# Fused transformer stack on one core: the second cross-attention gets folded query square sums, an earlier begin and a new order of its groups, its first group and its tail

## The chip, the cores and the metric

One core of one Trainium2 chip runs the whole program in one launch. The metric is the device time in microseconds (us). Below, PE is TensorE, DVE is VectorE, ACT is ScalarE, POOL is GpSimd and SP the engine that issues the DMAs.

## The reference

Six sublayers work on x (16 batches of 64 tokens, 512 wide), each followed by a layer norm of x plus its result. The fifth, the one this change is about, is a cross-attention with normalised queries and keys (cut):

```python
q = (hidden_states @ q_proj_w.T).reshape(B, Q, NUM_HEADS, HEAD_DIM).transpose(0, 2, 1, 3)
k = (cross_attention_states @ k_proj_w.T).reshape(B, KV, NUM_KV_HEADS, HEAD_DIM).transpose(0, 2, 1, 3)
v = (cross_attention_states @ v_proj_w.T).reshape(B, KV, NUM_KV_HEADS, HEAD_DIM).transpose(0, 2, 1, 3)
q = rmsnorm(q, q_norm_w)        # w * x * rsqrt(mean(x*x) + 1e-5), over the 128 of a head
k = rmsnorm(k, k_norm_w)
...
attn = jax.nn.softmax(scores + attention_mask, axis=-1)
out = jnp.einsum('bhqk,bhkd->bhqd', attn, v)
return out.transpose(0, 2, 1, 3).reshape(B, Q, NUM_HEADS * HEAD_DIM) @ o_proj_w.T
```

There are 32 query heads, 8 key/value heads of 128, keys and values come from a context `ctx_4096` (16 x 64 tokens) that doesn't depend on x. The fourth sublayer is a self-attention of the same size, the sixth a small gated mixture of low-rank experts.

## The kernel before

Stages follow one another: `attn0`, `xattn0`, `ffn0`, `attn1`, `xattn1` (the second cross-attention), `ffn1`. All values are float32. Large products are made as three matmuls of high and low parts (`mm3`, lines 263 to 265); small ones (scores, square sums) as true fp32 matmuls, each of which shows as two instructions.

An attention stage has 8 groups, one per key/value head with its 4 query heads. A group has 12 projection units, `U_0` to `U_11`. In `xattn1` the first four are key/value units (24 matmuls, context as the stationary side, 256 columns), which read only the context, and the other eight are query units (12 matmuls, 512 columns). `KT` transposes the normalised keys, `SQ` makes the square sums of the queries, `SC` scores of one pair of batches blocks, `TR`/`PT` carry the probabilities out to DRAM and back in turned order (DVE transpose, four DMAs out, one in, then a high/low split on ACT and DVE into `pth`, `ptl`), `PV` multiplies them with v, `WS` splits the output weights, `WO` (12 matmuls) projects a tile of 128 tokens out and adds it to X. Four pairs per group, numbered 0 to 3; eight `WO` tiles.

What sets the order is a string in `schedule`: each engine walks the same list and does its own share of every event, so the list is at once the order of PE, ACT and DVE. A dash behind an event means that it belongs to the group before. POOL and SP have orders of their own in `step` of `pool_attention` and `sp_attention`. Engines are tied by counting semaphores; each engine works in its own order, and a wait holds whatever stands behind it.

Square sums of the queries before: ACT writes the squares of a query unit to `sq` (line 690), PE multiplies eight 128 x 128 blocks of squares, as stationary side, with one column of ones (`square_sums`, line 576), DVE scales the eight columns (line 801), POOL takes the power -1/2 (line 971), and the scores are multiplied with it on DVE (line 816).

```python
for m in range(8):
    last = nc.tensor.matmul(pb[3][:, m:m + 1], sq[:, m, :], onecol[:, 0:1], start=True, stop=True)
```

Between `attn1` and `xattn1`, SP and POOL wait for the last addition to X (`stage_end`) before they load and split the first weights, and PE waits until all eight x tiles are normalised, transposed and split (`xt_ready`), although the key/value units don't read x. In the tail after the last group the remaining `PV` and `WO` run, each finished tile is normalised and transposed for the next stage, and POOL splits the weights of `ffn1` (line 1689).

## Time and profile before

| | us |
|---|---|
| median of 3 runs (2396.45 to 2406.70) | 2397.24 |
| profiled execution, its own time | 2401.77 |
| its span in the profile | 2400.0 |
| PE busy in the span | 2289.1 (95%) |
| DVE busy | 1206.0 (50%) |
| ACT busy | 780.5 (33%) |
| POOL busy | 765.6 (32%) |

Busy time of PE counts a matmul from its start to its modelled end, so matmuls overlap; the pace is read from the starts. The granted clock of PE is given as a share of full speed: 1.00 is the upper of two levels (2.4 GHz), 0.50 the lower (1.2 GHz), and a value between is a mix over the stretch. `[2.66 <-DVE otl L874]` behind a row: the engine sat idle for 2.66 us just before, and what ended it.

### The profile page before, as it was taken

The page shows a single profiled execution, that of the slowest core. Times are in us where ns is not written, and L with a number is a line of the kernel's source. Part 1 is how long each engine was busy: PE and PEld are TensorE (multiplying, and loading weights), DVE is VectorE, ACT ScalarE, POOL GpSimd, SP SyncE. Part 2 cuts the span into 40 slices and gives each one's busy share as a digit, 9 for nine tenths or more (in the row PEclk, how much of TensorE's full clock was granted, in tenths as well). Part 3 has the DMA queues.
Part 4 walks back from the last instruction along what each step waited for, and adds up shares of the span by engine and source line. Part 5 has one row for each costly group of instructions (what it writes and reads, how often), then busy time and mean ns, then how long its engine had stood idle before and what let it go on. Part 6 is the DMA issues. An engine that isn't in the chain of part 4 may idle for free. (4 is left out here: it accounts for less than half of the span.)

```text
span 2400.0 us, 34599 instructions
## 1 busy us (share of the span) xinstructions
PE 2289.1 (95%) x12210; PEld 1833.6 (76%) x12210; DVE 1206.0 (50%) x2052; ACT 780.5 (33%) x1475; POOL 765.6 (32%) x709
## 2 busy tenths in 40 slices
PE   8999999997999989998999999998899999999989
PEld 6888888875555557886788888887788888888867
DVE  3445544447677633334444444556345454544456
ACT  2233223223677731222322223332232233323321
POOL 4122222203333335444222222211443433333233
PEclk9999999998999999999999999999889999999989
DMA  4222222211000113311221222121121212211120
GB/s 160 80 66 60 76 79 79 57 45 32 18 18 11 64 70 123 105 52 54 81 80 50 67 75 78 56 53 49 59 80 54 57 48 79 67 43 53 53 75 36
DMA packets 120546, 152.43 MB, mean 64 GB/s; under 512 B 16272, under 2 KB 67984, under 8 KB 119952
## 3 DMA queue, kind: packets, MB, share of 16 engines
q1 hardware_dynamic: 120464, 151.33, 21.5%
q8 instruction: 52, 0.85, 0.1%
q14 instruction: 30, 0.25, 0.0%
HBM read 124.02 MB, written 27.26 MB: 63 GB/s over the span
## 5 line engine op out<-in xcount | busy, mean ns | idle before, releaser
L263 PE MATMUL banks<-xTh,wh 128*128 128x512 f32 x1024 | 418.7, 409 | 8.8 <-DVE xTl L1887 7.4
L265 PE MATMUL banks<-xTh,wl 128*128 128x512 f32 x1024 | 404.7, 395 | 0.0
L264 PE MATMUL banks<-xTl,wh 128*128 128x512 f32 x1024 | 403.6, 394 | 0.0
L263 PE MATMUL banks<-woh,oth 128*128 128x512 f32 x768 | 315.6, 411 | 23.3 <-DVE otl L874 16.4
L264 PE MATMUL banks<-wol,oth 128*128 128x512 f32 x768 | 302.5, 394 | 0.0
L961 POOL TENSOR_TENSOR sc_sb<-sc_sb,rs 128x512 f32<-128x512 f32 x96 | 104.3, 1090 | 621.1 <-DVE rs L837 621.1
L265 PE MATMUL banks<-woh,otl 128*128 128x512 f32 x768 | 302.1, 393 | 0.0
L880 DVE TENSOR_TENSOR X<-banks,X 128x512 f32<-128x512 f32 x192 | 132.7, 691 | 324.3 <-PE banks L265 323.9
L693 ACT ACTIVATE q_sb<-banks 128x512 f32<-128x512 f32 x192 | 114.5, 597 | 400.6 <-PE banks L265 400.6
L263 PEld LDWEIGHTS banks<-xTh,wh 128*128 128x128 f32 x1024 | 195.6, 191 | 51.0 <-issue 9.2
L265 PEld LDWEIGHTS banks<-xTh,wl 128*128 128x128 f32 x1024 | 194.9, 190 | 44.0
L264 PEld LDWEIGHTS banks<-xTl,wh 128*128 128x128 f32 x1024 | 195.9, 191 | 37.3
L564 PEld LDWEIGHTS banks<-k_sb,q_sb 128*128 128x128 f32 x1536 | 191.0, 198 | 19.0 <-ACT q_sb L693 6.7
L874 DVE TENSOR_TENSOR otl<-banks,oth 128x512 fp32r<-128x512 f32 x192 | 123.6, 686 | 158.6 <-ACT oth L733 158.6
L564 PE MATMUL banks<-k_sb,q_sb 128*128 128x64 f32 x1536 | 191.4, 279 | 9.5 <-ACT q_sb L693 4.1
L263 PEld LDWEIGHTS banks<-woh,oth 128*128 128x128 f32 x768 | 146.2, 190 | 69.3 <-DVE otl L874 17.9
L947 POOL TENSOR_TENSOR wl<-raw,wh 128x512 fp32r<-128x512 f32 x144 | 193.4, 1343 | 12.0
L945 POOL TENSOR_SCALAR wh<-raw 128x512 fp32r<-128x512 f32 x144 | 91.0, 632 | 314.1 <-DMA raw<-in_a_in 163.7
L265 PEld LDWEIGHTS banks<-woh,otl 128*128 128x128 f32 x768 | 145.9, 190 | 32.4
L264 PEld LDWEIGHTS banks<-wol,oth 128*128 128x128 f32 x768 | 146.4, 191 | 26.3
L733 ACT ACTIVATE oth<-banks 128x512 fp32r<-128x512 f32 x192 | 104.3, 596 | 124.1 <-PE banks L608 124.1
L690 ACT ACTIVATE sq<-banks 128x512 f32<-128x512 f32 x64 | 38.3, 598 | 242.7 <-PE banks L265 242.7
(208 smaller groups left out, 4039.9 us busy)
## 6 DMA issues: line engine op xcount, KB each, us to landing
raw<-in_a_in SPq DMA_DIRECT2D x144, 256.0 KB, 2.9
raw<-in_a_out SPq DMA_DIRECT2D x96, 256.0 KB, 2.7
turned<-pq SPq DMA_DIRECT2D x384, 64.0 KB, 2.0
pt<-turned SPq DMA_DIRECT2D x96, 256.0 KB, 2.9
f_q<-in_f_q SPq DMA_DIRECT2D x21, 512.0 KB, 3.9
f_s<-in_f_s SPq DMA_DIRECT2D x21, 512.0 KB, 5.3
X<-in_x SPq DMA_DIRECT2D x1, 2048.0 KB, 10.5
x_craw<-in_ctx SPq DMA_DIRECT2D x8, 256.0 KB, 2.7
```

The costliest lines, as they stand in the source:

```text
L263: nc.tensor.matmul(out, w_hi, x_hi, start=start, stop=False)
L264: nc.tensor.matmul(out, w_hi, x_lo, start=False, stop=False)
L265: return nc.tensor.matmul(out, w_lo, x_hi, start=False, stop=stop)
L564: last = nc.tensor.matmul(pb[2][:, (4 * c + m) * S:(4 * c + m + 1) * S], q_sb[:, 4 * (pair % 2) + m, c * P:(c + 1) * P], k_sb[:, col:col + S],
L690: nc.scalar.activation(sq[:, :, g % 2 * S:(g % 2 + 1) * S], bank[:, :].rearrange("p (c s) -> p c s", c=8), ACT.Square).then_inc(A["q_sq"], 1)
L693: nc.scalar.activation(q_sb[:, :, g * S:(g + 1) * S], bank[:, :].rearrange("p (c s) -> p c s", c=8), ACT.Copy).then_inc(A["q_free" if st.r ...
L733: nc.scalar.activation(oth[:, n % 2, :, 64 * b:64 * b + 64], PVB[b][:, :].rearrange("p (c s) -> p c s", c=8), ACT.Copy).then_inc(A["o_hi"], 1)
L874: nc.vector.tensor_tensor(otl[:, n % 2, :, half], PVB[b][:, :].rearrange("p (c s) -> p c s", c=8), f32(oth[:, n % 2, :, half]), ALU.subtra ...
L880: nc.vector.tensor_tensor(xtile(n), bank[:, :], xtile(n), ALU.add).then_inc(A["x_added"], 1)
L945: nc.gpsimd.tensor_scalar(hi, src, 1.0, 0.0, ALU.mult, ALU.add).then_inc(A["w_hi"], 1)
L947: nc.gpsimd.tensor_tensor(lo, src, f32(hi), ALU.subtract).then_inc(A["w_ready"], 1)
L961: nc.gpsimd.tensor_tensor(rows, rows, spread_rows(rs[:, pair, :]), ALU.mult).then_inc(A["p_ready"], 1)
```

## The change

1. **Square sums.** DVE transposes the squares in 32 x 32 blocks (`sq_turned`, 1024 elements a partition), reduces over 32 (`sq_part`, 32 a partition), and PE makes one fp32 matmul of a constant 128 x 128 matrix `fold` with these 32 columns. DVE then picks the columns that are a partition's own (`sq_pick`) and reduces by four. The event `SQ` is now the DVE transpose and reduce, and `SS` the matmul and the picking. Three small DVE instructions at the stage's begin build `fold` and its helpers.
2. **Begin.** `attn1`'s tail now holds `U_0` and `U_1` of `xattn1`'s first group, behind x tile 5's transposes and ahead of those of tiles 6 and 7, which go to other banks. SP loads the first weights as soon as `attn1` has used its own, POOL splits two chunks between norm roots, and only `U_4` waits for all x tiles.
3. **Order of a group.** In `xattn1`, `SC2`, `SC3` and `SS3` of a group run inside the next group, ahead of its `WO0`; the parts of the score work have events of their own (`SC` PE, `SD` DVE, `EX` ACT, `SU` DVE). The first group has one list for PE and another for ACT and DVE. POOL's and SP's orders follow, and in the tail the last scores move likewise; loads for `ffn1` are issued ahead of the last two turned pairs, and POOL's splits for it are put between the norm roots.
4. Two counters of the layer norm become one, and the counter of the outgoing transfers likewise, in all stages.

```diff
@@ schedule
     if rms:
-        ev = events("U_0 PT0- TR2- U_1 WS0- WS1- U_2 PV0- PT1- TR3- WS2- WS3- U_3 WO0- PV1- U_4 KT0 PT2- WO1- U_5 KT1 PV2- WO2- SQ0 "
-                    "U_6 PT3- U_7 WO3- SQ1 PV3- SC0 WO4- SC1 U_8 U_9 WO5- SQ2 TR0 U_10 U_11 TR1 WO6- SQ3 SC2 WO7- SC3")
+        ev = events("WS0- WS1- PT0- U_0 SS3- WS2- WS3- U_1 PV0- PT1- U_2 SC2- SD2- EX2- U_3 SU2- WO0- TR2- PV1- SC3- SD3- EX3- "
+                    "U_4 KT0 SU3- WO1- U_5 KT1 TR3- PT2- SQ0 U_6 PV2- SS0 U_7 WO2- PT3- SQ1 WO3- SS1 PV3- WO4- SC0 SD0 EX0 "
+                    "WO5- SU0 SC1 SD1 EX1 U_8 TR0 SU1 U_9 TR1 SQ2 WO6- U_10 SS2 U_11 SQ3 WO7-")
...
     if not project:
-        return events("PT0- TR2- PV0- WO6-- " + ("" if rms else "VT1- ") + "PT1- TR3- WO7-- WS0- WS1- PV1- WS2- WS3- WO0- PT2- WO1- "
+        if rms:
+            return events("PT0- PV0- WO6-- SS3- PT1- WO7-- WS0- WS1- SC2- SD2- WS2- WS3- EX2- SU2- PV1- SC3- TR2- WO0- SD3- EX3- "
+                          "SU3- WO1- TR3- WO2- PT2- WO3- PV2- WO4- PT3- WO5- PV3- WO6- WO7-")
...
+def first_group(rms, tensor):
+    if not rms:
+        return schedule(False, True, False)
+    if tensor:
+        return events("U_0 U_1 U_2 U_3 U_4 KT0 U_5 KT1 U_6 SS0 U_7 U_8 SC0 SS1 U_9 SC1 U_10 U_11 SS2")
+    return events("U_0 U_1 U_2 U_3 U_4 KT0 U_5 KT1 SQ0 U_6 SS0 U_7 SQ1 SS1 SD0 EX0 SU0 SD1 TR0 U_8 U_9 SQ2 EX1 SU1 TR1 "
+                  "U_10 U_11 SS2 SQ3")
@@ sp_attention
-            if st.before:
+            if st.name == "xattn1":
+                for name in ("w_ready", "wo_ready", "s_out"):
+                    sp.wait_ge(*st.at(name, 0))
+            elif st.before:
                 sp.wait_ge(*stage_end(st.before))
...
-                    if before and c in (1, 3):
+                    if before and c in (1, 3) and not st.rms:
                         move_out(i - 1, 2 + c // 2)
-                    if before and c in (2, 4):
+                    if before and c in (2, 4) and not st.rms:
                         move_in(i - 1, 1 + c // 2)
+                if before and st.rms:
+                    for pair in (2, 3):
+                        move_out(i - 1, pair)
+                        move_in(i - 1, pair)
@@ square_sums, PE
-                for m in range(8):
-                    last = nc.tensor.matmul(pb[3][:, m:m + 1], sq[:, m, :], onecol[:, 0:1], start=True, stop=True)
-                last.then_inc(A["ss_done"], 1)
+                nc.tensor.matmul(pb[3][:, 0:32], fold[:, 0:P], sq_part[:, j % 2, :], start=True,
+                                 stop=True).then_inc(A["ss_done"], 1)
@@ pe_attention, tail
+            if st.name == "attn1":
+                pe.wait_ge(const_set, 2)
+                pe.wait_ge(fs["c"], 4)
+                for u in range(2):
+                    pe.wait_ge(xt_ready, 8 * XT_NORMS["attn1"] + NT - 3 + u)
+                    pe_unit(pe, stages[2], 0, u)
@@ act_attention, query unit
+                    if isinstance(i, int) and (i, u) == (0, 8):
+                        st.need(act, "sc_done", 2)
-                    st.need(act, "ss_done", 4 * i + 2 * n + g // 2)
+                    st.need(act, "sq_turn", 4 * i + 2 * n + g // 2)
@@ dve_attention
+            def q_square_sums(i, j):
+                st.need(dve, "sq_sum", 4 * i + j)
+                st.need(dve, "q_sq", 8 * i + 2 * j + 2)
+                nc.vector.transpose(sq_turned[:, :, :].rearrange("p n d -> p (n d)"),
+                                    sq[:, :, :].rearrange("p m s -> p (m s)")).then_inc(A["sq_turn"], 1)
+                st.need(dve, "ss_done", 4 * i + j - 1)
+                st.need(dve, "sq_turn", 4 * i + j + 1)
+                nc.vector.tensor_reduce(sq_part[:, j % 2, :], sq_turned[:, :, :], AX_X, ALU.add).then_inc(A["sq_sum"], 1)
...
+                nc.vector.scalar_tensor_tensor(sq_pick[:, :, :], pb[3][:, 0:32].rearrange("p (m b) -> p m b", m=8), EPS,
+                                               own, ALU.add, ALU.mult).then_inc(A["sq_own"], 1)
@@ pool_attention, step of a stage with norms
                     if before:
+                        q_root(i - 1, 3)
+                    for n in range(3):
+                        k_root(i, n)
+                    if before:
                         normalise(i - 1, 2)
-                    k_root(i, 0)
-                    k_root(i, 1)
+                    if more:
+                        pool_split_chunk(pool, st, i + 1, 0)
+                        pool_split_chunk(pool, st, i + 1, 1)
+                    split_v(i, 0)
+                    k_root(i, 3)
                     if before:
                         normalise(i - 1, 3)
```

Three places in the orders show what the lists do.

DVE in a full group of `xattn1`, from the split of turned pair 2 (`ptl`) to the evacuation of pair 3 (`otl`). Before:

```order
L868 TENSOR_TENSOR ptl<-pt,pth 128x512
L880 TENSOR_TENSOR X<-banks,X 128x512
L789 TENSOR_SCALAR kst<-kst,rk 128x128 x2
L874 TENSOR_TENSOR otl<-banks,oth 128x8x64 x2
L880 TENSOR_TENSOR X<-banks,X 128x512
L801 TENSOR_SCALAR qms<-banks 128x2x4
L868 TENSOR_TENSOR ptl<-pt,pth 128x512
```

In the change:

```order
L924 TENSOR_TENSOR ptl<-pt,pth 128x512
L840 STREAM_TRANSPOSE sq_turned<-sq 128x1024
L844 TENSOR_REDUCE sq_part<-sq_turned 128x32
L930 TENSOR_TENSOR otl<-banks,oth 128x8x64 x2
L850 SCALAR_TENSOR_TENSOR sq_pick<-banks,quarter 128x32
L854 TENSOR_REDUCE qms<-sq_pick 128x2x4
L936 TENSOR_TENSOR X<-banks,X 128x512
L924 TENSOR_TENSOR ptl<-pt,pth 128x512
L840 STREAM_TRANSPOSE sq_turned<-sq 128x1024
L844 TENSOR_REDUCE sq_part<-sq_turned 128x32
```

One small DVE instruction (`qms`) became four, two of them long, and the two long ones stand directly behind the `ptl` of a pair.

POOL from the norm roots of `attn1`'s tail (`rstd`) to the first key roots (`rk`) of `xattn1` (`wh`, `wl`: the two halves of a weight chunk's split). Before:

```order
L341 TENSOR_TENSOR rstd<-var_eps,mhalf 128x1 x8
L945 TENSOR_SCALAR wh<-raw 128x512
L947 TENSOR_TENSOR wl<-raw,wh 128x512
...
L965 TENSOR_TENSOR rk<-kms,mhalf 128x2 x4
L945 TENSOR_SCALAR wh<-raw 128x512
```

In the change:

```order
L360 TENSOR_TENSOR rstd<-var_eps,mhalf 128x1 x3
L1014 TENSOR_SCALAR wh<-raw 128x512
L1016 TENSOR_TENSOR wl<-raw,wh 128x512
L360 TENSOR_TENSOR rstd<-var_eps,mhalf 128x1 x2
L1014 TENSOR_SCALAR wh<-raw 128x512
L1016 TENSOR_TENSOR wl<-raw,wh 128x512
L360 TENSOR_TENSOR rstd<-var_eps,mhalf 128x1 x3
...
L1035 TENSOR_TENSOR rk<-kms,mhalf 128x2 x3
L1014 TENSOR_SCALAR wh<-raw 128x512
```

Two of the six splits moved up between norm roots; of the four key roots three stand together, and the fourth now stands behind two splits of the next group and one of v.

DVE at the begin of `xattn1`'s tail. Before:

```order
L816 TENSOR_TENSOR sc_sb<-banks,rq 128x512
L819 TENSOR_TENSOR sc_sb<-sc_sb,bias 128x512
L829 TENSOR_REDUCE smax<-sc_sb 128x8
L831 TENSOR_TENSOR sc_sb<-sc_sb,smax 128x512
L835 TENSOR_REDUCE ssum<-sc_sb 128x8
L837 RECIPROCAL rs<-ssum 128x8
L835 TENSOR_REDUCE ssum<-sc_sb 128x8
L837 RECIPROCAL rs<-ssum 128x8
L868 TENSOR_TENSOR ptl<-pt,pth 128x512
```

In the change:

```order
L840 STREAM_TRANSPOSE sq_turned<-sq 128x1024
L844 TENSOR_REDUCE sq_part<-sq_turned 128x32
L924 TENSOR_TENSOR ptl<-pt,pth 128x512
L930 TENSOR_TENSOR otl<-banks,oth 128x8x64 x2
L936 TENSOR_TENSOR X<-banks,X 128x512
L850 SCALAR_TENSOR_TENSOR sq_pick<-banks,quarter 128x32
L854 TENSOR_REDUCE qms<-sq_pick 128x2x4
```

The first `ptl` of the tail stood behind the whole score work of pairs 2 and 3; now it stands behind the last transpose and reduce of squares alone.

## Rows read from the trace of the kernel before

**Rows 1.** Windows: stretch, PE, PEld, DVE, ACT, POOL busy, granted clock, DMA share, GB/s.

```profile
1689.00:1756.00 67.00, 60.77 (x328) 53.63 (x328) 19.07 (x42) 14.71 (x37) 34.53 (x35) 0.81 0.20 60
1756.00:1839.00 83.00, 82.18 (x470) 71.69 (x469) 39.20 (x76) 23.67 (x55) 28.80 (x28) 0.91 0.20 57
2100.00:2200.00 100.00, 97.22 (x604) 84.23 (x603) 44.78 (x87) 29.82 (x67) 36.17 (x34) 1.00 0.20 54
```

**Rows 2.** Timeline of PE and its weight loads in full groups: start, duration, instruction.

```profile
1951.10 1.84 PE L576 MATMUL banks<-onecol,sq 128*128 128x1 f32 x16
1952.80 0.49 PE L263 MATMUL banks<-xTh,wh 128*128 128x512 f32 x1
1958.38 0.39 PE L263 MATMUL banks<-woh,oth 128*128 128x512 f32 x1
...
1996.47 0.37 PE L263 MATMUL banks<-wh,cTh 128*128 128x256 f32 x1
2002.46 0.39 PE L263 MATMUL banks<-wh,cTh 128*128 128x256 f32 x1
2012.24 0.50 PE L263 MATMUL banks<-woh,oth 128*128 128x512 f32 x1 [2.66 <-DVE otl L874]
2014.03 0.19 PEld L263 LDWEIGHTS banks<-woh,oth 128*128 128x128 f32 x1 [0.57 <-DVE wol L883]
...
2230.29 1.89 PE L564 MATMUL banks<-k_sb,q_sb 128*128 128x64 f32 x16
2231.99 0.37 PE L263 MATMUL banks<-wh,cTh 128*128 128x256 f32 x1
```

**Rows 3.** Three DVE lines, 1690 to 2300: count, min/median/max ns.

```profile
L843 DVE STREAM_TRANSPOSE pq<-sc_sb x30: 701/710/714, 1740.7 to 2294.9; 128x512 f32<-128x512 f32 x30
L829 DVE TENSOR_REDUCE smax<-sc_sb x30: 685/686/687, 1726.8 to 2285.4; 128x8 f32<-128x512 f32 x30
L819 DVE TENSOR_TENSOR sc_sb<-sc_sb,bias x30: 691/692/1667, 1725.2 to 2284.6; 128x512 f32<-128x512 f32 x30
```

**Rows 4.** Timeline of ACT behind a query unit, and DVE's `ptl` after it.

```profile
2019.57 0.60 ACT L690 ACTIVATE sq<-banks 128x512 f32<-128x512 f32 x1 [1.85 <-PE banks L265]
2021.78 0.72 DVE L868 TENSOR_TENSOR ptl<-pt,pth 128x512 fp32r<-128x512 f32 x1 [2.78 <-ACT pth L729]
```

**Rows 5.** Timeline of PE: attn1's last x transposes, then first matmuls of xattn1's groups.

```profile
1680.25 0.60 PE L354 MATMUL banks<-ident,X 128*128 128x128 f32 x4
1689.49 0.55 PE L263 MATMUL banks<-wh,cTh 128*128 128x256 f32 x1 [4.53 <-POOL wl L947]
1756.08 0.56 PE L263 MATMUL banks<-wh,cTh 128*128 128x256 f32 x1
1839.52 0.37 PE L263 MATMUL banks<-wh,cTh 128*128 128x256 f32 x1
```

**Rows 6.** Timeline of POOL at xattn1's begin.

```profile
1682.35 0.78 POOL L341 TENSOR_TENSOR rstd<-var_eps,mhalf 128x1 f32<-128x1 f32 x1 [2.43 <-DVE var_eps L336]
1698.08 0.62 POOL L945 TENSOR_SCALAR wh<-raw 128x512 fp32r<-128x512 f32 x1 [2.88 <-DMA raw<-in_a_in]
1698.79 1.29 POOL L947 TENSOR_TENSOR wl<-raw,wh 128x512 fp32r<-128x512 f32 x1
1704.83 0.70 POOL L965 TENSOR_TENSOR rk<-kms,mhalf 128x2 f32<-128x2 f32 x1 [0.36 <-DVE kms L782]
```

**Rows 7.** Timeline of PE, DVE and SP from the last group into the tail.

```profile
2299.03 0.39 PE L265 MATMUL banks<-xTh,wl 128*128 128x512 f32 x1
2314.05 0.58 PE L608 MATMUL banks<-pth,vh 64*128 64x256 f32 x2 [5.45 <-DVE ptl L868]
2352.95 0.60 PE L354 MATMUL banks<-ident,X 128*128 128x128 f32 x4
...
2293.93 0.71 DVE L843 STREAM_TRANSPOSE pq<-sc_sb 128x512 f32<-128x512 f32 x1
2297.78 0.34 SPq L466 DMA_DIRECT2D pt<-turned  x1
```

More of the change, by code:

```diff
@@ L310, in program @@
         pt_in = [sem(f"pt_in{n}") for n in range(2)]
-        pq_out = [sem(f"pq_out{n}") for n in range(2)]
+        pq_out = sem("pq_out")
         turned = nc.dram_tensor("turned", (2, P, 512), F32, kind="Internal").ap()
@@ new lines, in pe_unit @@
+        def pe_unit(pe, st, i, u):
+            kind, g, n = st.units[u]
+            c = st.chunk_of(u)
+            if n == 0:
+                st.need(pe, "w_ready", 6 * i + c + 1)
+            if not (isinstance(i, int) and i == 0 and u < 2):
+                wait(pe, *st.unit_read(i, u - 2))
+            if st.name == "xattn1" and isinstance(i, int) and (i, u) == (0, 4):
+                pe.wait_ge(xt_ready, 8 * 3)
+            bank = pb[u % 2]
+            w = lambda k: (wh[:, c, k, :], wl[:, c, k, :])
+            if kind != "kv":
+                cols = slice(n * HALF, (n + 1) * HALF)
+                for k in range(KT):
+                    if st.name == "attn0" and isinstance(i, int) and u < 2 and k % 2 == 0:
+                        pe.wait_ge(x0_ready, 2 * u + k // 2 + 1)
+                    last = mm3(bank[:, :], w(k), (xTh[:, k, cols], xTl[:, k, cols]), k == 0, k == KT - 1)
+            else:
+                for m in range(2):
+                    t = 2 * n + m
+                    for k in range(KT):
+                        last = mm3(bank[:, 2 * m * HD:2 * (m + 1) * HD],
+                                   (cTh[:, k, t * P:(t + 1) * P], cTl[:, k, t * P:(t + 1) * P]),
+                                   (wh[:, 0:2, k, :], wl[:, 0:2, k, :]), k == 0, k == KT - 1)
+            last.then_inc(A["proj_done"], 1)
@@ L629, in run @@
                     if kind == "U_":
-                        unit(j, n)
+                        if not (st.name == "xattn1" and isinstance(j, int) and j == 0 and n < 2):
+                            pe_unit(pe, st, j, n)
                     elif kind == "SC":
                         scores(j, n)
-                    elif kind == "SQ":
+                    elif kind == "SS":
                         square_sums(j, n)
@@ L850, in run @@
                     if kind == "U_":
-                        unit(j, n)
+                        if not (st.name == "xattn1" and isinstance(j, int) and j == 0 and n < 2):
+                            dve_unit(dve, st, j, n)
                         if st.rms and 1 <= n < 5:
@@ L1013, in step @@
                         for c in range(2, 6):
-                            split_chunk(i + 1, c)
-            if st.before:
-                pool.wait_ge(*stage_end(st.before))
-            for c in range(2):
-                split_chunk(0, c)
+                            pool_split_chunk(pool, st, i + 1, c)
+            if st.name != "xattn1":
+                if st.before:
+                    pool.wait_ge(*stage_end(st.before))
+                for c in range(2):
+                    pool_split_chunk(pool, st, 0, c)
             if not st.before:
```

208 lines of the change are left out of this document (105 added, 103 removed).

## The prediction, made blind

> **What bounds the kernel now.** I read the windows first: in the steady part of `xattn1` PE is busy 97.22 of 100 us at full clock, DVE 44.78, ACT 29.82, POOL 36.17 [rows 1]. So the time is PE's own work plus PE's waits, and I went on with PE's timeline, reading starts, since the busy times overlap. Groups 2 to 7 begin 78.49 us apart on average ((2231.99 - 1839.52) / 5) [rows 2, 5]. Of one group the rows give: square sums 1.70 four times (16 instructions, 1951.10 to 1952.80); a score pair 1.70 as well (2230.29 to 2231.99), though each of its matmuls has 64 columns and not one; a query unit 2.79 (two in 5.58); a key/value unit 3.00 (two in 5.99); a wait of 2.66 before `WO0` and one of 0.57 within it [rows 2]. Beside the groups stand two poor stretches. From the end of attn1's last `WO` (1680.25) to group 1 pass 75.8 us, and group 1 takes 83.4 [rows 5]; over the first group the granted clock is 0.81, over the next 0.91, so parts of both ran at the lower level [rows 1]. And from the end of the last query unit (2299.4) to the last `WO`'s end (2352.95) pass 53.5 us, with PE waiting for `ptl` until 2314.05 [rows 7].
>
> **The steady groups.** Added on PE: four fold matmuls. Eight true fp32 matmuls cost 1.70 with 1 column and with 64, so one is 0.21 [rows 2]; it can't be under 0.1 (one of its two instructions) nor over 0.5. I take 0.21, since 32 columns lie between these rows. The Trainium skill ("FP8 and Floating Point Precision", TensorE Precision Notes) says that true fp32 takes four passes through the array; by 32 columns and its four passes one would be an estimated 0.05, and the sum 5 us lower over 32. The rows contradict a price by columns here, 1 and 64 costing the same, so the sum stays with them. Removed: 4 x (1.70 - 0.21) = 6.0. The wait of 2.66 and that of 0.57 go as well: between `PV0` and `WO0` stood one key/value unit (3.0), now stand two and a score pair (7.7), while `otl` came 5.7 (3.0 + 2.66) after `PV0`'s end, and the wanted `wol` are made ahead of `U_1`. That is 78.5 - 6.0 - 3.2 = 69.3 of work.
>
> What is late next is the squares' chain. Transposing and reducing 1024 elements costs twice the rows of 512: 2 x 0.61 to 0.71 each, 2.5 together with the semaphores [rows 3]. Bounds: 2.1 (the second half cheaper) and 4.5 (blocked once as the line that adds the mask, 1.67 against 0.69 [rows 3]). At `SS0`: from ACT's square of a query unit to `ptl` pass 2.2 [rows 4], `ptl` itself 0.7, then 2.5: the columns are there 5.4 after `U_5`. PE meanwhile has the last key transposes (0.4), `U_6` (2.8) and `PV2` (0.9): it waits 1.3. At `SS1` DVE has the addition of `WO2` (0.6), `ptl` (0.6) and 2.5, PE only `WO3` (2.7): it waits 1.0. `SS2` has `WO6` and `U_10` as cover with 1.8 to spare, `SS3` has `WO7` and `U_0` with 2.5 to spare. DVE's load rises by 4 x 2.7 to some 46 us of a group of 71.6, so it isn't the bound. The power on POOL and the masks follow later than before but have `U_0` to `U_2` above them; the turned pairs take 3.9 us from the DVE transpose to the issue of their way back [rows 7] and have 11 to 12 until they are wanted. SP has its loads grouped ahead of pairs 2 and 3, whose transposes come after them: nothing. Sum: 69.3 + 2.3 = 71.6, so 6.9 less. Five groups (2 to 6): **34.5**. Group 1 took 83.4, of which 83 x 0.09 = 7 is lost clock [rows 1]; I keep half of that, 71.6 + 3.5: **8**. Group 7 gains 4.5 on three square sums and 3.2 of waits, takes over a score pair twice (3.4) and `SS3` and waits 3.3: **1**.
>
> **The begin.** PE after attn1's last `WO`: transposes 0.35, `U_0` and `U_1` 6.0, transposes 0.7, then 32.7 (two key/value units 6.0, eight query units 22, key transposes 0.7, three folds 0.6, two score pairs 3.4). The POOL splits of chunks 0 and 1 (0.62 and 1.29, 1.93 with the pause) fit between norm roots, the last of which came 3.2 after its forerunner (2.43 idle and 0.78) [rows 6]. New waits: POOL is free at 1683.1 (last norm root) [rows 6], splits chunks 2 to 4 until 1688.9, waits 2.9 for the sixth chunk's data as before, splits it (1.9), makes three key roots (2.2), two splits and v's (5.8), and only then the fourth root: 1702.5, keys scaled 1703.1 [rows 6]. PE is at `KT1` by 1699.2: 3.9. The second half's query units overwrite what the first scores read, so ACT holds `U_8` until both scores are done and `EX0` is through; `U_10` waits 2.4 and `SS2` 0.6. The three setup instructions on DVE delay its copies to 1691, with `U_2` above them: nothing. Sum 0.35 + 6.0 + 0.7 + 32.7 + 6.9 = 46.7. The clock: before, 67 x 0.19 = 13 us were lost to it, about 12 of them in work [rows 1]. With fewer low stretches I take 5, so 51.7: **24**; with 12 it is 17, with none 29. The Trainium skill ("TensorE: Matmul & The Clock Gate", What's actually happening) says that the slow clock is the default and activity releases it. By that rule the wait before `KT1` can start a drop where PE has none in that place now; this case's rows show drops in exactly this stretch, so it is a rival below.
>
> **The tail.** Work: ten `WO` 27.5, four `PV` 3.7, two score pairs 3.4, a fold, five transposes 1.8: 36.6. The first `ptl` no longer stands behind the scores of pairs 2 and 3 but behind `SQ3`: 3.8 after the last unit. Then some 1.8 for `wol` before `WO0`, which DVE makes on both sides of pair 2's scores, and 1.7 before `WO3`, where pair 3's scores delay an addition. With 1 for clock: 44.9 against 53.5, **8.5**. The end of `ffn1`, from 2352.95 on, is as before; its loads go out earlier, its splits wait for nothing. Stages `attn0`, `xattn0`, `ffn0`, `attn1`: merged counters, nothing.
>
> **Sum.** 34.5 + 8 + 1 + 24 + 8.5 = 76. The profiled execution took 2401.77, so its like would take 2325.8; the median of the runs shown is 4.5 lower, hence **2321.2**.
>
> **Rivals.** *A, the squares' chain is late.* If transpose and reduce take 3.6 instead of 2.5, or `ptl` comes 1.1 later, `SS0` and `SS1` wait 1.1 more each in eight groups: 18 us, 2339. For it: they stand directly behind `ptl` on an engine that works in order. Against it: the narrow spread of both rows [rows 3]. *B, the begin gives back.* If half clock lasts over the new waits as it did over the old, begin and group 1 give 17 + 4.5 in place of 24 + 8: 2332; with waits of 3 us more at `KT1` and `U_10`, 2335. For it: 0.91 in group 1, where PE was busy 82.18 of 83 [rows 1], so a low clock outlasts its cause. *C, no wait at all behind the folds* and little lost clock: 18 + 8 lower, 2295. Against it: the counts above. *D, slower.* One mechanism: the transpose of 1024 elements over the whole partition is far from twice that of 512. If transpose and reduce take d, each us over 2.5 costs 16 in `SS0` and `SS1`, over 4.3 another 8 in `SS2` and over 5.0 another 8 in `SS3`. It decides at d = 6.0, where 16 x 3.5 + 8 x 1.7 + 8 x 1.0 = 78 eats the gain; at d = 7 it costs 72 + 22 + 16 = 110 and gives 2431. Against it: no transpose row above 0.714. *E, it doesn't do what it says:* PE finds its wait in the same places again (`otl` late before `WO0` in the new order as well), and only the 6.0 per group and the begin's 7 us gap are saved: 2397.2 - 48 - 7 = 2342.
>
> **Chances.** Forecast 0.55, A 0.14, B 0.13, C 0.09, E 0.04, D 0.03, no change from several of them 0.02. The range 2296 to 2352 takes in C (just), A, B and E with the fold's bounds (9 and -3 us) and leaves out D and half of C. About 0.5% (12 us) is what a measurement of this kernel can tell from no change. Faster by more than that: all but D and the last: 0.95; within 0.02; slower 0.03.
>
> **What would show it.** PE line of the fold: 64 instructions, pairs some 0.2 us apart. Groups 2 to 6 begin 71.6 apart, no wait before `WO0`, waits of about 1 before the folds of `SS0` and `SS1`, ended by `sq_part`. DVE's 128 x 1024 transpose and reduce at 1.2 to 1.3 each. `U_0` of `xattn1` begins 0.35 behind attn1's last `WO`; a wait near 4 before `KT1`, ended by the key scaling on DVE. Group 1 begins some 52 us after that `WO`. The tail's first `PV` about 4 behind the last unit. I am wrong if waits of PE over 2 stand in each group, if DVE's squares take over 3, or if the clock row stays at 0.5 for over 15 us after the begin.

## The result, and the profile after

The changed kernel took **2332.78 us** (median of 4 runs, 2330.51 to 2333.32) against 2396.84 for the kernel before on the same chip (4 runs, 2395.80 to 2406.70): ratio 0.9715, 95% interval 0.9691 to 0.9739. The quotient of the two medians is 0.9733, inside the interval. The forecast was 2321.2, the sign and the range hold, and the sum was 12 us too good. The table shows that this small distance is the rest of two larger errors of opposite sign. All times are PE starts of the two profiled executions (spans 2400.0 and 2331.0).

| part of the program | before | after | difference | forecast |
|---|---|---|---|---|
| start to attn1's last `WO` | 1680.25 | 1671.90 | -8.35 | 0 |
| from there to group 1 | 75.83 | 51.15 | -24.7 | -24 |
| group 1 | 83.44 | 75.40 | -8.0 | -8 |
| groups 2 to 6 | 392.47 | 357.95 | -34.5 | -34.5 |
| group 7, to the end of its last query unit | 67.4 | 67.2 | -0.2 | -1 |
| tail, from there to the last `WO` | 53.5 | 60.3 | **+6.8** | **-8.5** |
| ffn1 | 47.05 | 47.06 | 0 | 0 |

The changed kernel's page, its first lines:

```profile
span 2331.0 us, 33907 instructions
PE 2224.3 (95%) x11762; PEld 1769.8 (76%) x11762; DVE 1300.0 (56%) x2151; ACT 781.4 (34%) x1475; POOL 772.1 (33%) x709
```

Its windows over the begin, group 1, steady groups and the tail (columns as in [rows 1]):

```profile
1672.00:1723.00 51.00, 43.77 (x251) 37.68 (x249) 29.45 (x55) 14.59 (x37) 25.14 (x26) 0.93 0.17 47
1723.00:1798.00 75.00, 70.65 (x418) 60.49 (x416) 53.80 (x93) 24.86 (x56) 37.22 (x34) 0.98 0.31 81
2100.00:2200.00 100.00, 95.56 (x559) 80.41 (x558) 68.44 (x123) 34.14 (x76) 36.38 (x35) 1.00 0.19 50
2223.00:2284.00 61.00, 45.61 (x227) 36.85 (x226) 40.98 (x75) 13.84 (x25) 21.80 (x23) 0.86 0.19 57
```

In the steady part DVE rose from 44.78 [rows 1] to 68.44 of 100 us, above all by the squares. Begin and group 1 run at 0.93 and 0.98 of the clock in place of 0.81 and 0.91 [rows 1]. The last row is the surprise: PE is busy only 45.61 of 61 us in the tail.

PE's timeline, begin and one steady group (answers to [rows 5] and [rows 2]; the count at a row's end, here and below, is of the instructions inside the stretch that was asked for, so the second half of a pair or of a group of four can be missing):

```profile
1671.90 0.60 PE L373 MATMUL banks<-ident,X 128*128 128x128 f32 x4
1672.25 0.36 PE L283 MATMUL banks<-wh,cTh 128*128 128x256 f32 x1
1695.30 0.66 PE L619 MATMUL banks<-ident,kst 128*128 128x128 f32 x4 [3.98 <-DVE kst L829]
1715.69 0.50 PE L283 MATMUL banks<-xTh,wh 128*128 128x512 f32 x1 [2.68 <-ACT q_sb L733]
1723.05 0.37 PE L283 MATMUL banks<-wh,cTh 128*128 128x256 f32 x1
...
1904.70 0.41 PE L609 MATMUL banks<-sq_part,fold 128*128 128x32 f32 x2 [1.38 <-DVE sq_part L844]
1911.45 0.50 PE L283 MATMUL banks<-woh,oth 128*128 128x512 f32 x1 [0.78 <-DVE X L936]
...
1798.45 0.28 PE L283 MATMUL banks<-wh,cTh 128*128 128x256 f32 x1
2156.40 0.28 PE L283 MATMUL banks<-wh,cTh 128*128 128x256 f32 x1
```

`U_0` comes 0.35 behind attn1's last `WO`; the waits before `KT1` (forecast 3.9) and `U_10` (2.4) stand where they were put; `SS0` waits 1.38 (forecast 1.3; 0.90 to 1.39 over the groups). The second wait of the group is 0.78, not before the fold of `SS1` but before `WO3`, for the addition of `WO2`. The last two rows are the starts of groups 2 and 7: (2156.40 - 1798.45) / 5 = 71.59.

PE's timeline in the tail (answers to [rows 7]), and DVE's on the way to the first normalised tile:

```profile
2227.70 0.39 PE L641 MATMUL banks<-pth,vh 64*128 64x256 f32 x2 [3.96 <-DVE ptl L924]
2254.83 0.69 PE L373 MATMUL banks<-ident,X 128*128 128x128 f32 x2 [4.83 <-DVE X L365]
2264.36 0.50 PE L283 MATMUL banks<-woh,oth 128*128 128x512 f32 x1 [2.81 <-DVE otl L930]
2276.51 0.79 PE L283 MATMUL banks<-woh,oth 128*128 128x512 f32 x1 [2.95 <-DVE otl L930]
2283.94 0.60 PE L373 MATMUL banks<-ident,X 128*128 128x128 f32 x4
```

```profile
2246.33 0.69 DVE L351 BATCH_NORM_STATS2 st<-X 128x6 f32<-128x512 f32 x1
2247.46 0.69 DVE L869 TENSOR_TENSOR sc_sb<-banks,rq 128x512 f32<-128x512 f32 x1
...
2251.71 0.69 DVE L888 TENSOR_REDUCE ssum<-sc_sb 128x8 f32<-128x512 f32 x1 [0.70 <-ACT sc_sb L753]
...
2254.24 0.54 DVE L365 TENSOR_SCALAR X<-X,mv,rstd 128x512 f32<-128x512 f32 x1
```

Of the four waits only the first was forecast at its place and size; a fifth, of 0.73 before `WO7` of the older group, isn't shown. DVE has the statistics of tile 0 at 2246.33, POOL has its root by 2248.1 (2247.51 and 0.56), and DVE normalises it at 2254.24: between them lies the softmax of pair 3 (2247.46 to 2252.6). In the old list this softmax stood in the last group and ran ahead of the first `ptl`, as part of that wait of 5.45 [rows 7]; the new list moved it from in front of the first `PV` to in front of the first normalised tile.

The kernel before, over its own tail:

```profile
2299.00:2353.00 54.00, 44.27 (x239) 35.88 (x238) 38.03 (x72) 13.84 (x25) 21.17 (x22) 0.87 0.26 74
```

So the clock in this stretch was no higher before (0.87) than after (0.86).

### The profile page after: what moved, and what is told of

It is laid out like the page before. It is cut to its first block, busy times and chain, and to the rows that moved or that the text cites. A ratio compares the mean times of both kernels' runs of the same rounds, so it can differ in the third digit from the quotient of the medians.

```text
span 2331.0 us, 33907 instructions
## 1 busy us (share of the span) xinstructions
PE 2224.3 (95%) x11762; PEld 1769.8 (76%) x11762; DVE 1300.0 (56%) x2151; ACT 781.4 (34%) x1475; POOL 772.1 (33%) x709
## 4 chain that ended last, share of the span: by engine, by line
PE 80%; issue 7%; DVE 7%; POOL 4%; ACT 2%; DMA 0%; POOLq 0%; DVEq 0%; ACTq 0%; SPq 0%
PE banks L283 20%; PE banks L285 19%; PE banks L284 18%; PE banks L598 7%; PE banks L641 3%; PE banks L1279 3%; PE banks L1263 2%; POOL f_wl L1690 1%; PE banks L1245 1%; PE banks L1252 1%; PE banks L1215 1%; PE banks L1231 1%; POOL f_il L1698 1%; DVE st L351 1%; PE banks L1269 1%
## 5 line engine op out<-in xcount | busy, mean ns | idle before, releaser
L598 PEld LDWEIGHTS banks<-k_sb,q_sb 128*128 128x128 f32 x1536 | 186.0, 193 | 16.4 <-ACT q_sb L733 6.7
L598 PE MATMUL banks<-k_sb,q_sb 128*128 128x64 f32 x1536 | 185.0, 274 | 6.5 <-ACT q_sb L733 4.1
L753 ACT ACTIVATE sc_sb<-sc_sb 128x512 f32<-128x512 f32 x96 | 60.4, 631 | 226.5 <-DVE sc_sb L884 226.5
```

Source lines behind the costliest of these rows:

```text
L598: last = nc.tensor.matmul(pb[2][:, (4 * c + m) * S:(4 * c + m + 1) * S], q_sb[:, 4 * (pair % 2) + m, c * P:(c + 1) * P], k_sb[:, col:col + S],
```

## The experiments

Each kernel ran beside the kernel before on its own chip, so a whole is given as its ratio to that kernel (the changed kernel has 0.9715), and differences to the changed kernel in us are the difference of the ratios times 2397. With intervals of some 0.002 to each side such a difference is good to 7 us or so; for the smaller ones the reading rests on the stretches of the profiles. Within a profile, stretches are taken from PE's starts.

| kernel | median us | ratio, 95% interval | against the change |
|---|---|---|---|
| the change | 2332.78 | 0.9715 [0.9691, 0.9739] | |
| plain_tail_old | 2345.63 | 0.9768 [0.9751, 0.9784] | +12.7 |
| folds_in_old_order | 2377.94 | 0.9908 [0.9891, 0.9924] | +46 |
| begin_undone | 2340.62 | 0.9754 [0.9738, 0.9770] | +9.3 |
| reduce_twice | 2368.06 | 0.9869 [0.9853, 0.9886] | +36.9 |
| tail_covered | 2325.70 | 0.9688 [0.9670, 0.9705] | -6.5 |
| tail_scores_early | 2334.76 | 0.9726 [0.9706, 0.9746] | +2.6 |
| fourth_key_root_early | 2325.94 | 0.9688 [0.9670, 0.9706] | -6.5 |
| folds_later | 2323.09 | 0.9681 [0.9661, 0.9701] | -8.1 |
| tail_rebuilt | 2317.31 | 0.9655 [0.9633, 0.9677] | -14.4 |
| all_together | 2294.17 | 0.9561 [0.9543, 0.9579] | -36.9 |
| plain_tail_alone | 2388.95 | 0.9943 [0.9920, 0.9966] | |

### The 8 us that nobody forecast: plain_tail_old and plain_tail_alone

The diff shown ahead of the prediction leaves out a line of the change. In the list for the tails of the stages without norms, `PV0` had moved too:

```diff
-        return events("PT0- TR2- PV0- WO6-- " + ("" if rms else "VT1- ") + "PT1- TR3- WO7-- ...
+        return events("PT0- TR2- WO6-- VT1- PV0- PT1- TR3- WO7-- ...
```

The first of the two kernels undoes that line alone in the change; the second makes it alone in the kernel before.

> The changed kernel with one thing undone: in the tails of the stages without norms (attn0, attn1) PV0 stands again directly behind the key/value transposes, ahead of the older group's WO6. Theory (this line of the change is what made the part up to attn1's last WO 8.35 us shorter): that WO ends at 1680 again in place of 1671.90, PE waits some 3.7 us for ptl in both tails again where it now waits 0.46, and the whole is 8.3 us longer, about 2341. Rival (the merged semaphore counters, or a difference between executions): no change, 2333, attn1's last WO at 1672.

> The kernel before with one line of the change alone: in the tails of attn0 and attn1, PV0 behind the older group's WO6 and the v transposes. Theory (undoing it in the changed kernel cost 12.7 us, so it is worth as much here): the wait of 3.67 for ptl in each of these tails falls to 0.46, the half clock behind it goes, each tail is 5 to 6.5 us shorter, the whole 10 to 13 us shorter than before, ratio 0.9946 to 0.9958. Rival (the gain needs something else of the change beside it): under 5 us, ratio above 0.998.

PE's timeline, plain_tail_old: the first `PV` of attn0's tail, and the end of attn1's last `WO`.

```profile
529.62 0.58 PE L641 MATMUL banks<-pth,vh 64*128 64x256 f32 x2 [3.67 <-DVE ptl L924]
1686.06 0.60 PE L373 MATMUL banks<-ident,X 128*128 128x128 f32 x4
```

The same two places in plain_tail_alone:

```profile
529.53 0.39 PE L608 MATMUL banks<-pth,vh 64*128 64x256 f32 x2 [0.46 <-DVE ptl L868]
1671.51 0.60 PE L354 MATMUL banks<-ident,X 128*128 128x128 f32 x4
```

The old list brings the wait of 3.67 back in both tails, and the `WO` behind it takes 5.1 in place of 2.9, the lower clock level; it costs 12.7 us (14.2 by attn1's last `WO` in the profile). The new line alone saves 13.7 (2397 x 0.0057, interval 8 to 19). The theory's place was right and its size 4 us short, because the 8.35 of the table is a net value: the changed execution is already 2.7 us late by 70 us into the program, where the two kernels have the same instructions. Its first scores began 1.25 later (27.37 against 26.12), behind the first transfers of x (ACT waited 4.4 in all for one of its tiles against 3.2), and over 20 to 40 us the granted clock was 0.83 against 0.91. Of the profiles of all thirteen kernels eight show 0.83 in that window and five 0.91, whatever was changed later in the program. So differences of 2 to 3 us between the absolute starts of two profiles mean nothing here.

### What the fold is worth without the order: folds_in_old_order

The kernel before, with DVE's square sums and the fold (and one counter for the outgoing transfers), its group list kept but for the places of the square sums:

```diff
-  ... U_5 KT1 PV2- WO2- SQ0 U_6 PT3- U_7 WO3- SQ1 PV3- SC0 ... U_9 WO5- SQ2 TR0 U_10 U_11 TR1 WO6- SQ3 SC2 ...
+  ... U_5 KT1 SQ0 PV2- WO2- SS0 U_6 PT3- U_7 SQ1 WO3- PV3- SS1 SC0 ... U_9 SQ2 WO5- TR0 U_10 SS2 U_11 TR1 SQ3 WO6- SS3 SC2 ...
```

> The kernel before with the folded square sums alone: DVE's transpose and reduce start as soon as the squares are there, and the fold stands where the 16 matmuls stood or one step later; begin, order, masks and tail as before. Theory (the fold is worth 6.0 us a group and the new order next to nothing, 3.2 of waits taken away and 2.3 given): groups 2 to 6 begin some 74 apart (78.5 less 6.0, plus some 1.5 of waits for the chain at the last fold), the wait of 2.66 before WO0 stays, the whole is some 36 us shorter than before, about 2360, and group 7 with the tail is about 121 less 4, 117. Rival (without the new order the chain's waits eat what the fold saves): groups 77 or more apart, 2385 or more.

PE's timeline: two of the first group's folds, the wait before `WO0` in a full group, and the last fold that has no `WO` in front.

```profile
1714.28 0.30 PE L581 MATMUL banks<-sq_part,fold 128*128 128x32 f32 x1 [2.79 <-DVE sq_part L809]
1725.12 0.41 PE L581 MATMUL banks<-sq_part,fold 128*128 128x32 f32 x2 [3.29 <-DVE sq_part L809]
2000.76 0.50 PE L269 MATMUL banks<-woh,oth 128*128 128x512 f32 x1 [2.65 <-DVE otl L894]
2275.49 0.42 PE L581 MATMUL banks<-sq_part,fold 128*128 128x32 f32 x1 [3.36 <-DVE sq_part L809]
```

Full groups 2 to 6 begin 74.5 apart ((2207.79 - 1835.35) / 5): 4.0 less than before, as expected, with the 2.65 before `WO0` still there. But the whole fell by 22, not 36. In the first and the last group nothing covers DVE's chain: five folds wait 2.4 to 3.4, and the units behind them run partly at the lower clock level (the two behind the first fold took 7.3 us, against 5.6 at full clock). From attn1's last `WO` to group 1 this kernel takes 79.2, longer than before (75.8). In the full groups a part of the fold's gain is lost to the clock too: behind the same wait of 2.65 `WO0` takes 4.4 to 4.7 in five of six groups, where it takes 3.4 in the kernel before. So in steady groups the fold is worth 4.0 and the order 2.9 more; in the first group the fold without the order is a loss.

### The begin: begin_undone and fourth_key_root_early

```diff
 attn1's tail, PE and DVE
-                for u in range(2):
-                    pe_unit(pe, stages[2], 0, u)
...
 SP and POOL at xattn1's begin
+            if st.before:
+                sp.wait_ge(*stage_end(st.before))
```

> The changed kernel with only the start ahead of the last x transposes undone: U_0 and U_1 of xattn1, the splits of chunks 0 and 1 and SP's loads wait for attn1's end again; the new first group stays. Theory (the early start is worth the 7 us gap and some clock): from attn1's last WO to U_0 9.2 in place of 0.35, from that WO to group 1 some 61 in place of 51.2, of it up to 3 lost clock, the whole about 2343. Rival 1 (the new order of the first group brings the 24 alone, since POOL's sixth split and the wait before KT1 come at the same time whatever PE does): 51 to 53, 2335. Rival 2 (the early start brings nearly all 24, because the old gap let the clock fall for the first two groups): 72 or more and group 1 above 80, 2360.

```profile
1678.97 0.55 PE L283 MATMUL banks<-wh,cTh 128*128 128x256 f32 x1 [4.59 <-POOL wl L1006]
1701.45 0.33 PE L616 MATMUL banks<-ident,kst 128*128 128x128 f32 x1 [2.78 <-DVE kst L823]
```

`U_0` begins 9.3 behind attn1's last `WO` (1669.68) and group 1 58.0 behind it (1727.64), 6.8 later than in the change; the whole is 9.3 longer. That is between theory and rival 1. Undone, the early start costs 9.0 at `U_0`, but gives 1.2 back at `KT1`. So of the begin's 24.7 the early start holds 7, and by difference the folds with the new order of the first group the rest.

The other kernel lets POOL make the fourth key root ahead of the splits, in the first group:

```diff
-                    for n in range(3):
+                    for n in range(3 if before else 4):
                         k_root(i, n)
```

> The changed kernel with POOL's fourth key root of the first group ahead of the splits of the second group's chunks (in the first group only). Theory (POOL's queue is what makes PE wait 3.98 before KT1, and the half clock behind it costs some 1.5 more): the wait is below 0.5, from attn1's last WO to group 1 46 in place of 51.2, whole 2328. Rival (the splits, now 0.7 later, or the sixth chunk are late instead, or the wait turns up at the first fold): 50 or more, 2332.

```profile
1716.84 0.36 PE L283 MATMUL banks<-wh,cTh 128*128 128x256 f32 x1
```

No wait shows before `KT1` now, and group 1 begins 46.3 behind attn1's last `WO` (1670.50) in place of 51.2. The wait of 3.98 was POOL's order alone, and taking it away gave 4.8 with the clock behind it.

### The steady waits: reduce_twice and folds_later

```diff
                 st.need(dve, "sq_turn", 4 * i + j + 1)
+                nc.vector.tensor_reduce(sq_again[:, :], sq_turned[:, :, :], AX_X, ALU.add)
                 nc.vector.tensor_reduce(sq_part[:, j % 2, :], sq_turned[:, :, :], AX_X, ALU.add).then_inc(A["sq_sum"], 1)
```

> The changed kernel with a second 128x1024 reduce (into a tile that nobody reads) ahead of the one that makes the fold's columns, so that the squares' chain on DVE is 1.2 us longer, 32 times. Theory (the chain ends last before SS0 and SS1 and has 1 to 3 us to spare at SS2 and SS3): the waits at SS0 and SS1 grow by 1.2 each, groups 2 to 6 begin some 74.0 apart in place of 71.57, the whole is 18 to 22 us longer, about 2352. Rival 1 (only part of the waits is the chain's, the rest is the semaphores and the column load): under 1 us a group, 2340. Rival 2 (the chain has no spare anywhere): 4.9 a group, 76.5 apart, 2372.

One full group, PE:

```profile
1912.04 0.43 PE L620 MATMUL banks<-ident,kst 128*128 128x128 f32 x2 [0.74 <-DVE kst L830]
1918.39 0.29 PE L610 MATMUL banks<-sq_part,fold 128*128 128x32 f32 x1 [2.02 <-DVE sq_part L846]
1930.98 0.30 PE L610 MATMUL banks<-sq_part,fold 128*128 128x32 f32 x1 [1.15 <-DVE sq_part L846]
```

Groups 2 to 6 begin 75.6 apart, 4.0 more, not 2.4, and the whole is 36.9 longer: more than the theory, and less than rival 2 in the groups (76.5), about its size in the whole. Of the 4.3 us that the group shown is longer than one of the change, `SS1` has 1.1 (a new wait of 1.15) and `SS0` 0.6 (2.02 in place of 1.38), as the theory says or less. A new wait of 0.74 at `KT1`, with the step to the next unit, is 0.9. The last 1.6 stands in `U_7`, which has no wait and takes 4.4 where the change has 2.9: it runs at the lower clock level. PE over this `U_7`, and over `U_7` of one group of plain_tail_old:

```profile
1918.60:1923.07 4.47, 4.47 (x14) 0.62 0.22 58
1990.10:1994.50 4.40, 4.40 (x15) 0.61 0.09 35
```

With the wait before `SS0` at 2.0 to 2.5, `U_7` is slow (4.1 to 5.3) in six of seven full groups. The second row is from a kernel whose `SS0` waits as in the change. In seven such kernels (the change, plain_tail_old, begin_undone, tail_covered, tail_scores_early, fourth_key_root_early, tail_rebuilt) the wait is 0.8 to 1.4, and `U_7` is slow in 5 of 49 full groups, each 1.5 us longer than its neighbours, and each behind a wait of 1.38 or 1.39. So a wait of PE has a second price, the lower clock level in the unit behind it. It comes more often behind the longer wait, but not by the wait's length alone: the kernel before waits 2.4 to 2.8 in groups 2 to 7 without it. Added over a group, 1.2 us more on DVE's chain of squares, four times, cost 4.0 us.

```diff
-  ... U_6 PV2- SS0 U_7 WO2- PT3- SQ1 WO3- SS1 PV3- WO4- SC0 ...
+  ... U_6 PV2- U_7 SS0 WO2- PT3- SQ1 WO3- PV3- SS1 WO4- SC0 ...
```

> The changed kernel with SS0 behind U_7 in place of ahead of it, and SS1 behind PV3 in place of ahead of it, in the full groups. Theory (the wait before SS0 is DVE's chain of squares with only U_6 and PV2 as cover, and the one at WO3 and SS1 is DVE's queue in front of the addition of WO2): the wait of 1.38 before SS0 goes; the 0.78 before WO3 goes too if the ops of SS0 on DVE held WO2's addition up, else it stays; groups 2 to 6 begin 69.5 to 70.2 apart in place of 71.57, whole 2320 to 2323. Rival (the masks of pair 0 then wait for the roots on POOL, PE finds s_out late before SC1 or U_9): 71 or more, 2330.

```profile
1899.92 0.31 PE L609 MATMUL banks<-sq_part,fold 128*128 128x32 f32 x2
1903.82 0.50 PE L283 MATMUL banks<-woh,oth 128*128 128x512 f32 x1 [0.79 <-DVE X L936]
```

The wait before `SS0` is gone, groups 2 to 6 begin 70.1 apart ((2143.91 - 1793.33) / 5), and nothing waits for the masks. The 0.79 before `WO3` stayed, so `SS0`'s operations on DVE were not its cause. None of its full groups has a slow `U_7`.

### The tail: tail_covered, tail_scores_early and tail_rebuilt

```diff
-  ... SU3- WO1- TR3- WO2- PT2- WO3- PV2- WO4- PT3- WO5- PV3- WO6- WO7-
+  ... SU3- WO1- TR3- PT2- WO2- PV2- WO3- PT3- WO4- PV3- WO5- WO6- WO7-
```

> The changed kernel with PV2 ahead of WO3 in place of WO4, and PV3 ahead of WO5 in place of WO6, in the tail of xattn1. Theory (part of the tail's loss is that each of them is followed at once by the WO that needs its otl): the waits of 2.81 before WO4 and 2.95 before WO6 go, the transposed pairs are in time (pair 2's landed 2255, its PV would start near 2257), and the tail from the last unit to the last WO takes 54.6 in place of 60.4; whole 2327. Rival (DVE is the bound of this stretch, with the sums, statistics and normalisation of each tile in its queue): the waits move to the x transposes and the tail stays above 58.5.

```profile
2257.98 0.33 PE L373 MATMUL banks<-ident,X 128*128 128x128 f32 x1 [4.83 <-DVE X L365]
2280.07 0.49 PE L373 MATMUL banks<-ident,X 128*128 128x128 f32 x3
```

From the last unit to the last `WO` 53.1 (2280.07 less 2226.9, which is the first `PV`'s start of 2230.89 less its wait) in place of 60.3. Both waits for `otl` are gone (0.57 and 0.30 for `ptl` came instead, before the two `PV`), the 4.83 is as it was. In the old list each of these two `PV` had a `WO` of the pair before it standing behind it; the new list took that away.

The next kernel brings the softmax of pairs 2 and 3 forward, and POOL's power for pair 3 with it:

```diff
-  PT0- PV0- WO6-- SS3- PT1- WO7-- WS0- WS1- SC2- SD2- WS2- WS3- EX2- SU2- PV1- SC3- TR2- WO0- SD3- EX3- SU3- WO1- TR3- WO2- ...
+  PT0- SS3- SC2- PV0- SD2- EX2- WO6-- SU2- PT1- TR2- WO7-- SC3- SD3- EX3- WS0- WS1- PV1- SU3- WS2- WS3- TR3- WO0- WO1- WO2- ...
```

> The changed kernel with another order of xattn1's tail up to WO1: SS3 and the scores of pair 2 come first, those of pair 3 behind WO7 of the older group, and their masks, sums and transposes on DVE all end before WO0; POOL's power for pair 3 moves ahead of the norm roots. From WO2 on as changed. Theory (the tail lost because the softmax of pairs 2 and 3, some 3.6 us of DVE each, came out of the last group and now stands in DVE's queue between the additions and the statistics of tile 0, so that PE waits 4.83 for the first normalised tile): that wait goes, and with it the 0.73 before WO7; the tail takes 55 in place of 60.4, whole 2327. Rival 1 (the 4.83 is the norm chain's own length: add, statistics, root on POOL, normalise): it stays over 3.5, the tail 59 or more. Rival 2 (the scores ahead of PV0 lengthen the first wait, and the half clock after it costs more than is won): the tail 60 or more with a first wait over 5.

```profile
2227.40 0.30 PE L609 MATMUL banks<-sq_part,fold 128*128 128x32 f32 x1 [3.36 <-DVE sq_part L844]
2247.13 0.76 PE L283 MATMUL banks<-woh,oth 128*128 128x512 f32 x1 [4.04 <-DVE wol L939]
2258.36 0.38 PE L373 MATMUL banks<-ident,X 128*128 128x128 f32 x2
2286.49 0.38 PE L373 MATMUL banks<-ident,X 128*128 128x128 f32 x2
```

The 4.83 did go, so it was the softmax in front and not the length of the norm's chain. But 4.04 stands before `WO0`, since `wol` was now behind the softmax, the waits before `WO4` and `WO6` stayed (2.98 each), and so did one before `WO7` (0.87). The tail took 62.4, 2 more than the change, where 55 was expected: the waits are the same in sum (15.0 against 15.3), and the granted clock fell to 0.83. Moving work forward as such gains nothing where DVE's queue only changes which of its results is late. Hence the third kernel orders DVE's work by what PE wants next:

```diff
 last group
-  ... U_10 SS2 U_11 SQ3
+  ... U_10 SS2 PT0 U_11 SQ3
 tail
-  PT0- PV0- WO6-- SS3- PT1- WO7-- WS0- ...
+  PV0- WO6-- SS3- SC2- SD2- EX2- PT1- SU2- WO7-- TR2- SC3- WS0- WS1- PV1- WS2- WS3- SD3- WO0- EX3- SU3- WO1- TR3- PT2- WO2- PV2- WO3- PT3- WO4- PV3- WO5- WO6- WO7-
```

POOL's power for pair 3 stands ahead of the norm roots, as in the kernel before this one.

> The changed kernel with the tail of xattn1 in another order throughout, the rest as changed. The first ptl (PT0) is made ahead of U_11's square and the last square sums; PV0 and WO6 of the older group cover these sums, SS3 and SC2 follow; the splits of the output weights (WS) stand ahead of pair 3's softmax on DVE, not behind it as in the last try; pairs 2 and 3 are turned earlier; PV2 and PV3 have a WO between them and the WO that needs them. Theory (the tail is bound by DVE's queue, and what counts is which of its results PE wants next, not only how early the scores come): the first wait falls from 3.96 below 1, wol is waited for 1 or less in place of 4.04, the first x transposes 2 or less in place of 4.83, WO4 and WO6 not at all: last unit to last WO 43 to 47 in place of 60.2, whole 2316 to 2320. Rival (DVE has some 13 us of work between WO7 and the first normalised tile whatever the order, and PE 11 of cover, with the clock falling in each gap): the sum of the waits stays above 8 and the tail above 52, 2325 or more.

```profile
2221.51 0.39 PE L644 MATMUL banks<-pth,vh 64*128 64x256 f32 x2 [0.23 <-DVE ptl L927]
2233.44 0.39 PE L644 MATMUL banks<-pth,vh 64*128 64x256 f32 x2 [1.52 <-DVE ptl L927]
2236.80 0.76 PE L286 MATMUL banks<-woh,oth 128*128 128x512 f32 x1 [2.38 <-DVE wol L942]
2267.86 0.38 PE L376 MATMUL banks<-ident,X 128*128 128x128 f32 x2
```

46.6 us from the last unit (2221.28) to the last `WO`, with DVE as busy as before (40.09 us, the change 40.98). The waits add up to 5.3 in place of 15.3, and the granted clock is 0.93. Three of them the expectation did not put right: those for the second `ptl` (1.52), for `wol` (2.38 instead of 1 or less) and before `PV2` (0.98, not shown); the tile's wait is below what shows as one, and `WO4` and `WO6` wait for nothing.

### All together

```diff
-  ... U_6 PV2- SS0 U_7 WO2- PT3- SQ1 WO3- SS1 PV3- WO4- SC0 ...
+  ... U_6 PV2- WO2- SS0 PT3- U_7 SQ1 WO3- PV3- SS1 WO4- SC0 ...
```

with the edits of fourth_key_root_early and tail_rebuilt.

> The changed kernel with three edits together: the fourth key root early in the first group, the rebuilt tail, and in the full groups WO2 ahead of U_7 with SS0 behind WO2 and SS1 behind PV3. Theory: 4.8 in the begin, 13 to 17 in the tail, and in the groups the 1.38 before SS0 and the 0.78 before WO3 (WO2 and WO3 share a bank, and with U_7 between them the addition of WO2 is hidden): groups 2 to 6 begin 69.3 to 69.6 apart, 7 groups by 2.1. Whole 2332.8 - 4.8 - 15 - 15 = 2298, between 2292 and 2304. Rival for the 0.78 (not the shared bank but DVE's ptl ahead of the addition holds WO3): it stays or moves to SS0, groups 70.1 apart, 2303. Rival for the whole (one gain opens the other's wait, since all three load DVE and POOL at the same places): above 2310.

```profile
1748.05 0.33 PE L622 MATMUL banks<-ident,kst 128*128 128x128 f32 x1 [0.85 <-DVE kst L832]
1758.13 0.39 PE L286 MATMUL banks<-woh,oth 128*128 128x512 f32 x1
1788.13 0.28 PE L286 MATMUL banks<-wh,cTh 128*128 128x256 f32 x1
2133.93 0.28 PE L286 MATMUL banks<-wh,cTh 128*128 128x256 f32 x1
```

2294.17 us, 4.4% below the kernel before and 1.6% below the change, clear of both intervals. The wait before `WO3` (here at 1758.13, with `U_7` ahead) is gone, so it was the shared bank: in the full groups all `WO` write one bank, `WO3` may not write before `WO2` has been added to X, and with nothing between them PE waits out that addition. (A second bank was not tried.) The 0.85 before a key transpose in group 1 comes with the early key root: fourth_key_root_early has 0.89 there. Groups 3 to 6 have no wait at all. Groups 2 to 6 begin 69.2 apart ((2133.93 - 1788.13) / 5). Within what such differences are good for, the gains add up in full: 36.9 against 14.4 + 6.5 + 8.1 and 7 x 0.79, 34.5 in all.

## Why the prediction was right, and where it was wrong

**Steady groups: right, with one place wrong.** 34.5 forecast, 34.5 measured. The wait before `SS0` is 1.38 (forecast 1.3), and none stands before `WO0`, so rival E falls. The 1.0 at `SS1` showed as 0.78 before `WO3` and 0.2 in the fold. Its reason in the text (DVE's queue ahead of the fold) holds as far as it goes: DVE has the columns 3.8 after it begins the addition of `WO2` (two instructions of 0.6, then 2.6), against 3.7 forecast, and reduce_twice made it a wait of 1.15. What was not seen is the shared bank, which holds PE before `WO3` already and so hides most of it. all_together, which has neither wait, gives 69.2 a group, the 69.3 of work in the sum. The DVE lines came as bounded: the transpose of 1024 elements 1.24, the reduce 1.22 (medians of 32). That is 1.74 and 1.78 times the 512-element rows [rows 3]. The 2.5 of the forecast was right, but not as twice these rows: its 0.61 stands in none of them, and twice 0.71 and 0.69 is 2.8. So A and D fall on their conditions (3.6 and 6.0 for the two together), and C on the wait of 1.38. The Trainium skill ("Vector Engine (DVE) Microarchitecture Reference", 3.8) calls the transpose pipelined at one element per cycle and lane; the trace has 0.53 us for 512 more elements, and no run here shows how long a cycle of DVE is.

**The fold: its price was right on average.** From a fold's start to the next matmul pass 0.14 at `SS2` and `SS3`, 0.24 at `SS0` and 0.34 at `SS1`, where PE comes out of a wait: 0.21 in the mean, as forecast. The Trainium skill's four passes ("FP8 and Floating Point Precision", TensorE Precision Notes) gave an estimated 0.05 for 32 columns; even the 0.14 is above that, and each fold is two instructions in the profile, not four.

**Begin and group 1: right, one reason wrong.** 24 and 8 forecast, 24.7 and 8.0 measured. The waits before `KT1` (3.98, forecast 3.9) and `U_10` (2.68, forecast 2.4) are in place, and the clock went from 0.81 to 0.93, so B did not come. What B fears does happen on a small scale: after the wait of 3.98 the matmuls of `U_6` stand 0.43 apart in place of 0.23, the lower level. The Trainium skill ("TensorE: Matmul & The Clock Gate", What's actually happening) has the throttled state as the default, which activity releases; this row agrees. Group 1 is 3.8 longer than a steady group, but not by clock alone, as the sum had it. `SS3` of the first group waits 2.11 there for `sq_part`: the prediction counted `WO7` among its cover, and the first group has no `WO`. The unit behind it takes 4.27 in place of 3.05, the clock's share.

**The tail: wrong by 15.** The step that failed is the sum "44.9 against 53.5". Its work (36.6) and its first wait (3.8, measured 3.96) were right. Forecast behind them were 1.8 before `WO0`, 1.7 before `WO3` and 1 of clock. Measured were 0.73 before `WO7`, none before `WO0`, 4.83 before the first x transposes (directly ahead of `WO3`), 2.81 before `WO4` and 2.95 before `WO6`: 15.3 of waits in place of 7.3. And the clock was 0.86, so that about 8 were lost to it and to transitions, not 1. So 8 of the 15 are waits and 7 are clock. The clock's 1 was given without a reason: the kernel before has 0.87 over its own tail, 54 x 0.13 = 7 us. Of the waits, two were mis-sized or left out. Pair 3's softmax in DVE's queue was seen as the delay of one addition (1.7), not as standing in front of tile 0's normalisation. And the wait for `otl` behind `PV2` and `PV3` was not asked for, though the group's part of the same prediction reckons with just that delay. That both are causes is shown: tail_scores_early took away the 4.83 (and made other waits), tail_covered the two for `otl` (7 us). tail_rebuilt took away all three and most of the first wait (13.7 of 60.3). In the last two the lost clock shrank with the waits (0.90 and 0.93).

**Upstream: wrong by 8 here, 13 by the runs.** The step was "Stages `attn0`, `xattn0`, `ffn0`, `attn1`: merged counters, nothing". The merged counters did cost nothing that shows. What it lacks is the moved `PV0` in the lists of `attn0` and `attn1`, worth 12.7 undone and 13.7 alone, each good to 6 or 7 us. Without it the change would have saved some 51 us, and the forecast of 76 would have been 25 too good: 15 of it in the tail, 2.7 at the program's start, 4.5 because the profiled execution of before lay that far above its median, and 3 that no single part holds. So the total was nearly right by luck: of the 64 us measured, some 13 come from a place that the prediction did not name.

## What to carry to other kernels

An instruction that is made cheap on one engine is not free until its chain on the other has cover: the same fold gave 4.0 us per steady group without a new order, but cost time in the first group, where nothing stood in front of it. When an order list is rewritten, ask for each result which instruction wants it next and what stands between, at the two ends of the loop most of all: behind each `PV` that needs an evacuation, and between two writers of one bank. A wait of PE costs more than its length, for the unit behind it may run at the lower clock level: price a tight stretch with the clock that the trace of before shows in it. And compare forecast and measurement part by part along the program before calling a forecast right.
